# Four places of a four-block transformer kernel reordered: per-tile statistics, a later bias, keys ahead of states, and a bias moved within GpSimd's slot

## What is computed

```
x = layernorm(x + attn16(x))        # block 1: 16 heads of 16, softmax over all 512 keys,
                                    #   values scaled by a small gate network, @ Wproj + bproj
x = layernorm(x + slots(x))         # block 2: 16 slots, 16 experts (two 256x1024, one 1024x256 each)
x = layernorm(x + retention(x))     # block 3: S = g*S + k v^T ; y = q S ; group norm ; @ Wo
x = layernorm(x + local(x))         # block 4: 2 layers of windowed attention (8 heads of 64, window 128)
                                    #   + gated MLP on h = shift_token(x):  x = x + h2 @ w2 + b2
```

## Time and profile before

| | |
|---|---|
| median of 3 runs | 2361.08 us (2354.46 to 2362.95) |
| profiled execution | 2357.87 us, of it the span 2356.1 us |
| PE busy | 2254.7 us (96%) |
| DVE / ACT / POOL busy | 1639.4 / 1254.6 / 731.8 us |
| blocks 1, 2, 3, 4 (by PE's work) | about 0 to 565, to 838, to 1023, to 2356 us |

### The profile page before, as it was taken

How to read it: one execution, slowest core, us unless ns; L and a number is a source line. 1 busy time by engine, 2 the same in 40 slices (tenths; PEclk the granted TensorE clock), 3 DMA queues, 4 the chain that set the end, 5 groups by cost and what they waited for, 6 DMA issues and landing times.

```text
span 2356.1 us, 42487 instructions
## 1 busy us (share of the span) xinstructions
PE 2254.7 (96%) x16306; PEld 1322.2 (56%) x16306; DVE 1639.4 (70%) x4252; ACT 1254.6 (53%) x2823; POOL 731.8 (31%) x730
## 2 busy tenths in 40 slices
PE   8999999999898989988899999999999999999998
PEld 3333333333632867765566666666666666666665
DVE  6788888886510846667876777677767777787764
ACT  4666666665221532237666556556665666566640
POOL 3343233321020411134433333343333333333321
PEclk7999999999998999999999999999999999999999
DMA  7444333334279020000000000000001000000001
GB/s 237 144 148 118 118 118 114 117 105 164 94 321 396 2 90 19 19 28 21 6 6 6 1 6 6 6 1 32 15 5 53 6 15 22 13 14 23 21 23 39
DMA packets 68617, 158.44 MB, mean 67 GB/s; under 512 B 6256, under 2 KB 49120, under 8 KB 63936
## 3 DMA queue, kind: packets, MB, share of 16 engines
q1 hardware_dynamic: 65856, 146.55, 17.5%
q0 software_dynamic: 2560, 9.18, 1.7%
HBM read 116.39 MB, written 35.13 MB: 64 GB/s over the span
## 4 chain that ended last, share of the span: by engine, by line
PE 74%; DVE 15%; ACT 4%; DMA 3%; issue 2%; POOL 1%; SPq 0%; POOLq 0%; DVEq 0%; ACTq 0%
PE banks L2046 10%; PE banks L2024 7%; PE banks L1905 6%; PE banks L1919 5%; PE banks L232 5%; PE banks L272 4%; PE banks L245 4%; PE banks L2006 3%; PE banks L1949 3%; PE banks L1964 3%; DVE arena L481 2%; DVE arena L2589 2%; PE banks L1931 2%; DMA arena<-in_e_Wg 2%; PE banks L1428 1%
## 5 line engine op out<-in xcount | busy, mean ns | idle before, releaser
L481 DVE TENSOR_REDUCE arena<-banks 128x1 f32<-128x512 f32 x512 | 323.4, 681 | 72.1 <-PE banks L232 72.0
L393 ACT ACTIVATE arena<-banks 128x512 f32<-128x512 f32 x512 | 280.2, 595 | 146.3 <-PE banks L245 144.2
L2046 PE MATMUL banks<-arena 128*128 128x512 f32 x640 | 293.2, 594 | 1.0 <-DVE arena L2231 1.0
L2128 ACT ACTIVATE arena<-arena 128x256 f32<-128x256 f32 (+1 forms) x512 | 286.5, 562 | 5.0 <-DVE arena L2237 4.5
L2384 POOL TENSOR_TENSOR arena<-arena 128x512 f32<-128x512 f32 x128 | 162.7, 1271 | 380.0 <-DVE arena L2268 380.0
L1905 PE MATMUL banks<-arena 128*128 128x512 f32 x512 | 241.5, 594 | 2.8 <-DVE arena L2268 2.8
L232 PE MATMUL banks<-arena 96*128 96x512 bf16 x512 | 204.8, 403 | 17.5 <-DVE arena L481 14.3
L245 PE MATMUL banks<-arena 128*128 128x512 bf16 x512 | 195.0, 387 | 2.8 <-ACT arena L393 2.2
L2380 POOL TENSOR_TENSOR arena<-arena 128x16 f32<-128x16 f32 x64 | 189.4, 2959 | 5.3
L2100 ACT ACTIVATE arena<-arena 128x256 f32<-128x256 f32 (+1 forms) x256 | 102.1, 471 | 163.2 <-DVE arena L2213 163.2
L2046 PEld LDWEIGHTS banks<-arena 128*128 128x128 f32 x640 | 115.5, 190 | 126.7 <-issue 116.5
(11 more groups left out here) (302 smaller groups left out, 4238.1 us busy)
## 6 DMA issues: line engine op xcount, KB each, us to landing
arena<-in_e_W SPq DMA_DIRECT2D x16, 2048.0 KB, 16.2
arena<-stacks SPq DMA_DIRECT2D x64, 384.0 KB, 4.5
arena<-in_e_Wg SPq DMA_DIRECT2D x8, 2048.0 KB, 17.8
stacks<-arena SPq DMA_DIRECT2D x32, 384.0 KB, 2.5
stacks<-arena SPq DMA_DIRECT2D x32, 256.0 KB, 2.8
arena<-dens POOLq DMA_DIRECT2D x32, 256.0 KB, 4.6
arena<-in_xT SPq DMA_DIRECT2D x8, 512.0 KB, 7.9
stacks<-arena SPq DMA_DIRECT2D x32, 128.0 KB, 2.5
```

The costliest lines, as they stand in the source:

```text
L393: e.activation(ex[:, j], self.psum[:, self.exp_bank1(k)], ACT.Exp).then_inc(s["a_e"], 1)
L481: e.tensor_reduce(split(self.maxima[n % 2][:, 0:16], TILES, UNIT)[:, t, j:j + 1], self.psum[:, k % 3], AX.X, ALU.max, negate=True).then_in ...
L2046: i = e.matmul(bank, weights[:, c], self.hT[:, c], start=c == 0, stop=c == 1)
L2128: k = e.activation(pr[:, h, at:], pr[:, h, at:], ACT.Exp, bias=mx[:, h:h + 1], scale=rn[:, h:h + 1], accum_out=den[:, h:h + 1])
```

## The change

1. Block 1: the bn_stats of a tile follows the addition of that tile; the task "norm" keeps only the four bn_aggr.
2. Block 1: GpSimd's bias for sequence b waits for `a_prep` b+3, the end of VectorE's shift in the same step.
3. Block 3: PE projects half 0 of the keys ahead of the two state products instead of behind them.
4. Block 3, last sequence: VectorE computes the coefficients ahead of the state masks, and masks the second `own` ahead of the sums of y0.
5. Block 4, slot 2: ScalarE copies the first half of a transpose ahead of dividing the weights.
6. Block 4: GpSimd's bias comes between the pow and the two rotary additions of its slot, where it came behind them.

```diff
@@ vector1_task
         elif kind == "proj": ...
             e.tensor_tensor(x, x, bank[:, 0:CH], ALU.add).then_inc(s["a_x"], 1)
+            w.wait_ge("a_x", 4 * unit + index + 1)
+            e.bn_stats(split(self.norm1[unit % 2][:, 0:24], TILES, 6)[:, index], x).then_inc(own.up(), 1)
         elif kind == "norm":
-            self.stats_of(e, w, "a_x", [4 * unit + t + 1 for t in range(TILES)], self.norm1[unit % 2], self.x_nat[:, unit], s["a_stat"])
+            stats, mv = ...
+            w.wait_ge(own.sem, own.n)
+            for t in range(TILES):
+                i = e.bn_aggr(mv[:, t], stats[:, t])
+            i.then_inc(s["a_stat"], 1)
@@ gpsimd1_task
         elif kind == "bias":
             w.wait_ge("n%d" % unit, 16)
             w.wait_ge("l_small", 16)
+            w.wait_ge("a_prep", unit + LAG + 1)
@@ tensor3_slot
         if b is not None:
+            if a is not None:
+                self.tensor3_project(e, w, "k", a, 0)
             self.tensor3_state(e, w, b, 0)
             self.tensor3_state(e, w, b, 1)
+        elif a is not None:
+            self.tensor3_project(e, w, "k", a, 0)
         if a is not None:
-            self.tensor3_project(e, w, "k", a, 0)
             self.tensor3_project(e, w, "k", a, 1)
@@ vector3
         self.vector3_own(e, w, b, 0)
+        self.vector3_coefficients(e, w, b - 1)
         self.vector3_state(e, w, b, 0)
         self.vector3_state(e, w, b, 1)
-        self.vector3_coefficients(e, w, b - 1)
         self.vector4_lengths(e, w, 0)
+        self.vector3_own(e, w, b, 1)
         self.vector3_sums(e, w, b, 0)
-        self.vector3_own(e, w, b, 1)
@@ scalar4
+            if n == 2:
+                self.scalar3_turn(e, w, SEQS - 2, 0)
             if c is not None:
                 self.scalar4_divide(e, w, c)
-            if n == 2:
-                self.scalar3_turn(e, w, SEQS - 2, 0)
@@ gpsimd4
             if n < TILES4:
                 self.gpsimd4_tile(e, w, n)
+            else:
+                self.gpsimd4_bias(e, w, n)
@@ gpsimd4_mlp: the branch r == 1 (slot == MLP_STEP * m + MLP_FIRST + 1) becomes gpsimd4_bias
-            elif r == 1:
-                w.wait_ge("m_shifted", 32 * (m + 1)) ...
-                e.tensor_tensor(x, x, repeated(self.S(f"b_2{l}"), TILES), ALU.add).then_inc(s["m_bias"], 1)
```

More of the change, by code:

```diff
@@ L555, in vector1_task @@
             e.tensor_tensor(x, x, bank[:, 0:CH], ALU.add).then_inc(s["a_x"], 1)
+            w.wait_ge("a_x", 4 * unit + index + 1)
+            e.bn_stats(split(self.norm1[unit % 2][:, 0:24], TILES, 6)[:, index], x).then_inc(own.up(), 1)
         elif kind == "norm":
-            self.stats_of(e, w, "a_x", [4 * unit + t + 1 for t in range(TILES)], self.norm1[unit % 2], self.x_nat[:, unit], s["a_stat"])
+            stats, mv = split(self.norm1[unit % 2][:, 0:24], TILES, 6), split(self.norm1[unit % 2][:, 24:32], TILES, 2)
+            w.wait_ge(own.sem, own.n)
+            for t in range(TILES):
+                i = e.bn_aggr(mv[:, t], stats[:, t])
+            i.then_inc(s["a_stat"], 1)
         elif kind == "apply":
@@ L2425, in gpsimd4_mlp, with gpsimd4_bias @@
                 self.rsqrt(e, w, self.norm4[1], s["f_rstd"])
+    def gpsimd4_bias(self, e, w, slot):
+        for m in range(MLPS):
+            l, b = divmod(m, SEQS)
+            if slot == MLP_STEP * m + MLP_FIRST + 1:
+                x = self.x_nat[:, b]
+                w.wait_ge("m_shifted", 32 * (m + 1))
+                w.wait_ge("m_half", 2 * m + 2)
+                w.wait_ge("m_norm", m + 1)
+                w.wait_ge("l_late", 16)
+                e.tensor_tensor(x, x, repeated(self.S(f"b_2{l}"), TILES), ALU.add).then_inc(self.s["m_bias"], 1)
     def sync4(self, e, w):
```

## The result

Six runs of the changed kernel have a median of 2372.18 us (2368.99 to 2376.07); six of the kernel before, 2353.86. The ratio is 1.0072, interval 1.0056 to 1.0089. The time lies in the predicted range (2344 to 2384), 6 us above the 2366. By the ratio it is slower by more than 0.5%, a case to which 0.28 was given and not the 0.51 of "same"; on the prediction's own scale, which starts from 2361.08 us and puts "slower" above 2372.9, the 2372.18 would just still be "same". As a change, 5 to 6 us were forecast, and 14 us came in the profiled executions and 17 to 18 in the medians. The kernel before measured 2356.5 to 2357.9 us beside the experiments, so its 2353.86 here is some 3 us low; against those the changed kernel is 0.6 to 0.7% slower.

A forecast was written before the change was run, and what follows sets the result against it. TensorE, busy in 96% of the span, was taken to bound the kernel. Won 15.3 us, lost 21.5: 2364.1 us from the profiled 2357.87, or 2367.3 by the runs' median; 2366 was taken, range 2344 to 2384.

The forecast's parts named there:

- same: The case of a time between 2349.3 and 2372.9 us, within about 0.5% of the kernel before; chance 0.51.
- 1.65 us per bias: Block 4, slots 12 to 60: the moved bias holds VectorE's negation, so w1 starts 1.65 us late; 13 times, 21.5 us lost.
- slot 8: Block 4: TensorE's wait of 2.29 us falls to about 0.8; 1.5 us won plus 1.0 for the clock, 2.5.
- first rival: Block 4: the bias misses the first negation and meets only the second; nothing is lost, 2346 us; chance 0.24.
- clock rival: Block 4: the new 1.7 us wait also lowers TensorE's clock; 21 us more, 2387, or 2377 in half the slots; chance 0.14.
- +8.1 - 0.6: Block 1's bias behind the shift: casts give back 4.2 us and the clock 2.4 + 1.5; a late reciprocal root costs 0.6.
- the stall of L532: Block 1: a VectorE cast beside GpSimd's bias lasts 2.33 instead of 0.17 us; 2.16 us to be won.
- unit 5's term: Block 1: the second held cast, 2.20 us at 139.59, gives back 2.03 us and the clock 1.5.
- the term for bias 7: Block 1: once, the waiting bias delays the norm's reciprocal root, which reaches VectorE up to 0.8 us late; minus 0.6 us.
- what queues behind the waiting bias: Block 1, GpSimd: splits of queries and keys, due about a step later, so not charged.
- The wait moved to y0: Block 3: in six slots TensorE's wait moves from the states to y0, 0.05 us won; slot 1 wins 0.78; together 1.1.
- third rival: Block 1: extra bn_stats cost more than 0.2 us each and the clock returns nothing; only 5 us won, 2377; chance 0.12.

The follow-up runs named there:

- e1: The changed kernel with block 4's bias back in its old place behind the rotary additions; 2350.97 us, 0.9965 of the kernel before.
- e2: The kernel before with only block 4's bias moved behind the pow; 2373.29 us, 1.0063 of the kernel before.
- e8: The changed kernel, but block 4's bias waits for both negations of its slot; 2345.07 us, 0.9958 of the kernel before.
- e9: The changed kernel, but block 4's bias waits for only the first of its slot's two negations; 2351.94 us, 0.9976 of the kernel before.
- e3: The kernel before with only block 1's bias moved behind the shift; 2361.08 us, 1.0017 of the kernel before.
- e12: The changed kernel with block 4's bias behind both negations and no wait in block 1's bias; 2342.89 us, 0.9942 of the kernel before.
- e4: The kernel before with only block 1's statistics by tile; 2352.90 us, 0.9973 of the kernel before.
- e7: The kernel before with only the inverse sums one step sooner; 2359.16 us, 1.0013 of the kernel before.
- e5: As e1, and block 1's bias 7 no longer waits for the shift; 2347.74 us, 0.9966 of the kernel before.
- e6: As e5, and the inverse sums are computed and sent one step sooner; 2349.16 us, 0.9968 of the kernel before.
- e10: As e8, with bias 7 free of the shift and sequence 6's load in unit 4, not 5; 2346.24 us, 0.9950 of the kernel before.

## Why the prediction was right or wrong

**Edit 6: right in mechanism and size.** 1.65 us per bias was forecast, 1.68 came; 13 of these less the 19.6 us of the stage leave 2.2 for slot 8, where 2.5 was forecast. Of the 1.68 TensorE is idle for 1.23; the rest is not idle time (L1975 lasts 1.32 us at that place, where its counterpart lasted 1.04). e1 and e2 show that it is this edit, e8 that it is the meeting with the negations and not the bias's place behind the pow as such. The first rival turned on 0.2 us of start time: e9 made it by hand, and its claim of slack behind the second negation holds (0.9 us in 13 slots). The clock rival is out: 1.23 us of waiting left the clock at 1.00.

**Edit 2: wrong, +8.1 - 0.6 forecast and about 4 us lost (e3, interval 1.4 to 6.6).** e12 agrees in that the wait wins nothing: without it the median is no higher. Three steps failed.

First, it took the stall of L532, 2.33 us, as one of every execution; unit 3's stall is a coincidence of one. The bias starts when its load lands, at 102.10, 0.04 us ahead of the cast. In the four other traces without the wait (e2, e4, e7, e12) it starts behind the cast, and unit 3 lasts 17.0 to 17.6 us, not 21.8. The closest is e4, where 0.12 us decide:

```profile
102.34 0.17 DVE L532 CAST arena<-arena 128x16 bf16<-128x16 f32 x1
...
102.46 2.35 POOL L667 TENSOR_TENSOR arena<-arena 128x1024 f32<-128x1024 f32 x1 [3.37 <-DMA arena<-in_x]
```

So 4.6 of the 8.1 us (the cast's 2.16 and 2.4 for the clock) were there to be won in one trace of five. Only unit 5's term is steady (17.3 to 19.0 us without the wait, 15.2 to 15.4 with it).

Second, the term for bias 7 ahead of the norm's reciprocal root, "minus 0.6", was mis-sized sevenfold. The root is 3.1 us late, not 0.8, and what I left out is what the normalisation then meets: GpSimd's cuts, beside which four operations take 3.83 instead of 1.66 us. With the clock unit 8 costs 4.3 us (21.82 against 17.49 of unit 12 in the same trace; e5 brings it to 17.50). It is a meeting of VectorE and GpSimd like that of edit 6, looked for in one place and not in the other.

Third, what queues behind the waiting bias was taken to be splits with time to spare, and the transfers of GpSimd and SyncE were left out. With the bias behind the shift and units 3 and 5 short, the inverse sums are written 3.1 to 3.5 us behind a fetch of queries and keys (5.5 to 6.8 us without the wait), the write takes 3.5 to 4.8 us (2.5 to 2.7), and the next fetch follows 0.8 to 2.1 us behind the broadcast (2.9 to 3.1). VectorE then waits 2.8 to 5.1 us in all eight such traces that have the inverse in its old place, and 0 to 0.9 in the four without. What grows is the time of these transfers: VectorE is ready for its product 10.2 us after the write's issue in the eight and after 10.4 to 10.8 in the four, while write and broadcast together take 13.0 to 15.4 us against 10.2 to 11.7. That the fetches lengthen them is argued from this order and from e6, where the write stands 0.7 us behind a fetch and takes 5.5 us; no run moved the fetches. The load of sequence 6 beside the broadcast does not suffice (e12 issues it 0.9 us ahead of the broadcast, and VectorE does not wait) and is not needed (e10). Which transfers do it stays open.

**Edit 1: right.** 3.7 us forecast; the trace has 6 x 0.86 won and 6 x 0.16 lost, 4.2 us, and e4's interval is 3.5 to 9.2.

**Edits 3 to 5: right.** The wait moved to y0, as worked out, and 0.57 us of it is left in a slot, where about 0.65 was forecast; block 3 won 1.9 us for 1.1 forecast. Edit 4 won nothing, as said: the waits of 1.35 and 2.70 us are both there after the change. In the last stage 0.5 was forecast and 2.0 seen, of which 1.5 is clock: behind the wait of 2.70 us the clock fell in the kernel before and not in the changed one. e12, where it fell, takes 123.0 us to the kernel before's 123.5, which is the 0.5 forecast for edit 5. Behind the wait in the changed kernel:

```profile
1033.52:1040.00 6.48, 6.47 (x66) 5.78 (x67) 6.27 (x16) 1.20 (x2) 2.54 (x3) 1.00 0.00 0
```

The third rival, "block 1 gives little", had 0.12 and happened, by late transfers and a late normalisation instead of the extra bn_stats. That the time still lies in the range is in part luck. The range is 40 us wide, and it starts from a median of 2361.08 us, where six runs of the kernel before gave 2353.86; the missing 10 us of block 1 fitted into it.

## What to carry to other kernels

An operation that is moved on GpSimd is priced by the VectorE operations on SBUF alone that run within it at the new place, and again at the end of every delay that it causes. Here such operations were held: two-input ones, casts, and the normalisation's scalings. A negation that started 0.2 us into the bias cost 1.7 us in each of 13 slots, and a window in which VectorE reads PSUM cost nothing. A stall seen in one execution, next to a transfer's landing, may be a coincidence until a second trace shows it. And before a stretch is made shorter, look for the wait on a transfer behind it that has no margin: it can take back what was won.

## What the runs showed of the hardware

The broadcast (four transfers of 256 KB behind a write of 32 KB) has little margin even in the steady part: in five of the twelve traces with the inverse in its old place VectorE waits for it by 0.2 us or less, or not at all, in each of sequences 1 to 5. Where it comes 1.2 to 1.9 us late (seven cases), TensorE waits 2.0 to 2.8 us, and in five of the seven a stretch of 3.4 or 6.8 us at the lower clock begins within 1.5 us of that wait's end. Such a case makes a unit 1.8 to 5.7 us longer. Equal kernels differ by more: the twelve runs of e4 reach from 2345 to 2359 us, of which only the slowest was profiled, so how much of this the broadcasts do is not shown.

The same wait of 2.70 us in the last sequence was followed by 3.4 us at 1.2 GHz in seven of the fourteen traces and by full speed in the other seven.
